# A fused decoder block in fp32: finer loads and stores, the weight loads on another queue, a new order, and bf16 products of constants that nobody reads

## The reference, cut to what matters

```
x = x + attention(layernorm(x))      # 16 query heads of 32, one shared key and value head, causal
x = x + xattn(layernorm(x), f, ctx)  # two int8-quantised products per batch element, silu between them
x = x + ffn(layernorm(x))            # 512 -> 1376 -> 512 gated, plus low-rank terms:
    gate = x@W_gate + lora(x) + sum_e w_e * (x@A_e)@B_e     # same for up and for down
    w    = top 2 of 8 experts by sigmoid(x@W_router) + bias, normalised
```

## Time and profile before

| | us |
|---|---|
| median of 3 runs | 1038.27 |
| lowest, highest | 1030.74, 1038.53 |
| the profiled execution, whole | 1036.64 |
| its span in the trace | 1034.7 |
| PE, PEld, DVE busy in the span | 931.2, 665.7, 618.7 |
| ACT, POOL busy in the span | 313.5, 248.5 |
| mean granted TensorE clock | 0.927 |

### The profile page before, as it was taken

How to read it: one execution, slowest core, us unless ns; L and a number is a source line. 1 busy time by engine, 2 the same in 40 slices (tenths; PEclk the granted TensorE clock), 3 DMA queues, 4 the chain that set the end, 5 groups by cost and what they waited for, 6 DMA issues and landing times.

```text
span 1034.7 us, 13134 instructions
## 1 busy us (share of the span) xinstructions
PE 931.2 (90%) x5214; PEld 665.7 (64%) x5214; DVE 618.7 (60%) x865; ACT 313.5 (30%) x496; POOL 248.5 (24%) x217
## 2 busy tenths in 40 slices
PE   1898898587998989999999899999979999779996
PEld 1665446454546767767677676766757787668884
DVE  2355667877568668676566686966467574532222
ACT  2423443254342313534314026343222422121110
POOL 3612331412524003123220040321303123001110
PEclk9957889697679999999999999999989999989999
DMA  7863682433645753356426733362354545445542
GB/s 262 284 209 106 241 275 74 117 113 109 235 156 215 208 178 120 123 201 241 173 72 186 208 115 129 124 236 98 127 191 153 190 163 202 153 150 199 178 163 87
DMA packets 42657, 174.98 MB, mean 169 GB/s; under 512 B 5148, under 2 KB 7964, under 8 KB 32612
## 3 DMA queue, kind: packets, MB, share of 16 engines
q1 hardware_dynamic: 42596, 174.14, 49.1%
HBM read 127.52 MB, written 33.75 MB: 156 GB/s over the span
## 4 chain that ended last, share of the span: by engine, by line
PE 72%; DVE 14%; issue 4%; SPq 4%; DMA 2%; ACT 2%; POOL 1%; POOLq 0%; DVEq 0%; ACTq 0%
PE ring L932 12%; PE ring L933 11%; PE ring L934 11%; PE av L1039 4%; PE slot L1025 4%; PE den L1039 3%; PE ring L1170 3%; PE slot L1005 3%; DVE negm L1288 3%; SPq L576 3%; PE slot L1108 2%; PE slot L932 2%; PE slot L934 2%; PE slot L1023 2%; PE slot L933 2%
## 5 line engine op out<-in xcount | busy, mean ns | idle before, releaser
L932 PE MATMUL ring<-xT_h,gu 128*128 128x512 f32 x352 | 144.7, 411 | 9.1 <-DMA gu<-gu_parts 8.5
L735 POOL TENSOR_TENSOR hd_l<-hd,hd_h 128x512 fp32r<-128x512 f32 x44 | 57.5, 1306 | 384.2 <-ACT hd_h L908 384.2
L1288 DVE TENSOR_REDUCE negm<-slot 128x4 f32<-128x512 f32 (+2 forms) x96 | 98.9, 1044 | 68.1 <-PE slot L1005 67.7
L933 PE MATMUL ring<-xT_l,gu 128*128 128x512 f32 x352 | 139.6, 397 | 0.0
L934 PE MATMUL ring<-xT_h,gu 128*128 128x512 f32 x352 | 139.5, 396 | 0.0
L810 ACT ACTIVATE probs<-slot 128x256 f32<-128x256 f32 (+3 forms) x128 | 85.6, 700 | 90.6 <-PE slot L1025 90.5
L932 PEld LDWEIGHTS ring<-xT_h,gu 128*128 128x128 f32 x352 | 67.6, 192 | 25.2 <-issue 10.9
L934 PEld LDWEIGHTS ring<-xT_h,gu 128*128 128x128 f32 x352 | 67.5, 192 | 15.1
L1025 PE MATMUL slot<-qst,kst 98*128 98x128 f32 (+3 forms) x256 | 77.1, 396 | 0.0
L933 PEld LDWEIGHTS ring<-xT_l,gu 128*128 128x128 f32 x352 | 67.8, 193 | 12.2
L1005 PE MATMUL slot<-kst,qst 96*128 96x128 f32 (+3 forms) x256 | 74.1, 401 | 0.0
(11 more groups left out here) (194 smaller groups left out, 1768.5 us busy)
## 6 DMA issues: line engine op xcount, KB each, us to landing
gu<-gu_parts SPq DMA_DIRECT2D x44, 1280.0 KB, 5.5
dn<-dn_parts SPq DMA_DIRECT2D x12, 1728.0 KB, 7.9
gu_parts<-gu SPq DMA_DIRECT2D x11, 1280.0 KB, 5.7
qst<-qT_h SPq DMA_DIRECT2D x64, 128.0 KB, 2.5
raw_gu<-gu SPq DMA_DIRECT2D x11, 640.0 KB, 7.4
dn_parts<-dn SPq DMA_DIRECT2D x11, 576.0 KB, 3.3
dn<-dn_parts SPq DMA_DIRECT2D x4, 1152.0 KB, 5.3
x_in<-x SPq DMA_DIRECT2D x4, 1024.0 KB, 6.3
```

Source lines behind the costliest of these rows:

```text
L735: pool.tensor_tensor(hd_l[:, i, :], hd[:, i, :], hd_h[:, i, :].bitcast(F32), ALU.subtract).then_inc(hd_lo.sem, 1)
L932: pe.matmul(out_, w_hi_, m_hi_, start=start, stop=False, skip_group_check=True)
L933: pe.matmul(out_, w_hi_, m_lo_, start=False, stop=False, skip_group_check=True)
L1288: dve.tensor_reduce(negm[:, h0:h0 + heads, qt].rearrange("p (a c) -> p a c", a=2), slots[SLOT["max", b, g, i]][:, :, 0:heads // 2 * n].rea ...
```

## The change

- **fill.** 94 new steps of PE alone issue 1 to 9 bf16 matmuls each of the identity with the 128x384 masks into the ring bank that comes next, 303 in all: 117 in 38 steps of FIRST, 136 in 37 of SECOND, none in STEADY, 50 in 19 of LAST. Nobody reads the result, as the next tenant of the bank starts its sum anew. A fill waits, as the next claim would, for the reader of that bank.
- **Loads.** The first load of x is two halves with a semaphore each, so are the later ones. c_loaded counts the constants and the masks alone; five small loads raise v_loaded, which is waited for where they are first used.
- **gu loads.** From tile 2 on they are issued by ACT, in step hid, behind its copy hd_h. Before, SP issued them.
- **Stores.** total is stored in four pieces of 256 KB, each when its rows are done.
- **Steps.** The low-rank products of gate and up are a step k = 4 of their own. w_turn and y stand behind the first four steps of gate of tile 0, not ahead of them, and w_turn takes a slot, not a ring bank.
- **Order.** The four strings are new.

```diff
@@ -78,6 +78,13 @@
         if place in self.left:
             eng.wait_ge(*self.left[place])
         self.left[place] = (signal.sem, value)
+        return self.places[place]
+
+    def upcoming(self, eng):
+
+        place = self.n % 2
+        if place in self.left:
+            eng.wait_ge(*self.left[place])
         return self.places[place]
 
 
@@ -207,16 +214,16 @@
     yield ("router", b)
     yield ("logits", b)
     yield ("route", b)
-    yield ("w_turn", b)
-    yield ("y", b)
     behind = []
     for f in range(FT):
         for name in ("gate", "up"):
-            for k in range(KT):
+            for k in range(KT + 1):
+                if f == 0 and name == "gate" and k == KT:
+                    yield ("w_turn", b)
+                    yield ("y", b)
                 yield (name, b, f, k)
                 if name == "up" and k == 1:
                     yield ("gated", b, f)
-        yield ("gu_load", FT * b + f + 2)
         yield ("hid", b, f)
         yield from behind
         behind = []
@@ -225,10 +232,11 @@
                 behind = [("ad", b, s)]
                 if s == len(SEGMENTS) - 1:
                     behind += [("yd", b)]
-                behind += [("down", b, s, tt, j) for tt in range(TT) for j in range(len(tiles))]
+                for tt in range(TT):
+                    behind += [("down", b, s, tt, j) for j in range(len(tiles))]
+                    behind += [("store", b, tt)] * (s == len(SEGMENTS) - 1)
                 behind += [("dn_load", len(SEGMENTS) * b + s + 1)]
     yield from behind
-    yield ("store", b)
 
 
 def preparation_steps():
@@ -240,36 +248,37 @@
         yield ("prep_gu", f)
         yield ("prep_dn", f)
         yield ("prep_out", f)
-    yield ("gu_load", 0)
-    yield ("gu_load", 1)
+    yield ("gu_first",)
     yield ("dn_load", 0)
 
 
 
 
 FIRST = (
-    "AAAAAAAAWWAAAAAAAAWAWAWAAAAAAAWWAAAAAAAAAAAAAAAAAAAAWAWAAAAWAAAAAAAAAAAAAWAAAAAAWWWAAAAAAAAAAAAAAAWAAAAAAAAWAA"
...
+    "41AAAA14AA1AAAAA19AAWAWAA1WAWA4AAA4AW1AA414A1AA1WWA1A4AAA4AAAAAAAAAAAA1AWA1AAAA9AWAWAAAAA94AAAAAAA1AWAWA4AAWAW"
...
 SECOND = (
-    "LAALLWLLALWAALLLAALLALWLAALLALLLLLLLALAALALLAAALLLAALLLWLWLLLWALLLLLLAAALAAALAAAAAALAAALLLAAAAAALAAALLALLLAALL"
...
+    "LLAAW4LLLAAWLLALAALLLWAL1AA41LALL9LLLLAAL99A9LALLA4LA9LA9LL4L1AALALLWLLL1LWWALL11L4LALLLAAALAA1AAAAALA11AALLAL"
...
 STEADY = (
-    "FFFFAFALFFLAFFAALAFFFFFAFLFFAAAFFAFALFFFFFAFAFFFFFFFLFFFLLFFFFFFFAFFALFAAFFFFAFFLLFLAFFFLFAFFFLALFFLFLFAFLLFFF"
...
+    "AFALFLFAFFFAFFAFAFFLAFLFFFALFFAAFAFFFAFFAFFFFLFFFFAFFLFFFFLFFAFFFFAFAFFLAFFFFALFLFFFFLFFALFAFFLALFLFALFFFLALLA"
...
 LAST = (
-    "FFFFFFLLLFFFFLLFFFFFFLLFFLFFFFLFFFFLFFLLFFFFFFLFFLFFFFLFLFLFFLFFFFLLFLLLFFFFFFFFLFFFFLLFLLFLFFFLFLFFFFLFFFLLFF"
...
+    "1FF1FLLFF1F414FFFF9LLFLFFLFFLFFFF1LFFFFFFFLFFFFLFFFFFLFFFLLFLLF1FFLFFLFFLFFFFLFLFLLFFFLFFLFFFLLLFFFLFFLLFFLFFF"
...
 
 
 def in_order():
     streams = {"A": [s for b in range(BATCH) for s in attention_steps(b)], "L": [s for b in range(BATCH) for s in layer_steps(b)],
                "F": [s for b in range(BATCH) for s in feed_forward_steps(b)], "W": list(preparation_steps())}
     left = {name: iter(steps) for name, steps in streams.items()}
-    order = [next(left[name]) for name in FIRST + SECOND + (BATCH - 2) * STEADY + LAST] + list(left["F"])
-    assert len(order) == sum(len(steps) for steps in streams.values())
+    order = [("fill", int(name)) if name.isdigit() else next(left[name])
+             for name in FIRST + SECOND + (BATCH - 2) * STEADY + LAST] + list(left["F"])
+    assert len([step for step in order if step[0] != "fill"]) == sum(len(steps) for steps in streams.values())
     return order
 
 
@@ -483,15 +492,16 @@
...
-            sp.dma_start(x_in[:, :, :], rows_of(x[0])).then_inc(x_loaded.sem, 16)
+            for h in range(2):
+                sp.dma_start(x_in[:, 2 * h:2 * h + 2, :], rows_of(x[0])[:, 2 * h:2 * h + 2, :]).then_inc(x_loaded[h].sem, 16)
             sp.dma_start(cst[:, :], ap["consts"][:, 0, :]).then_inc(c_loaded.sem, 16)
             sp.dma_start(masks[:, :, :], ap["consts"][:, 1:3, :]).then_inc(c_loaded.sem, 16)
...
-            sp.dma_start(bias_bc[:, :], ap["expert_bias"].partition_broadcast(P)).then_inc(c_loaded.sem, 16)
...
+            sp.dma_start(bias_bc[:, :], ap["expert_bias"].partition_broadcast(P)).then_inc(v_loaded.sem, 16)
...
@@ -515,16 +525,11 @@
                 if f + 2 < FT:
                     sp.dma_start(raw_dn[f % 2][:, :], ap["dn"][f + 2]).then_inc(raw_dn_loaded[f % 2].sem, 16)
 
-            def gu_load(n):
-                if n >= BATCH * FT:
-                    return
-                i, _, f = gu_tile(n)
-                if n < 2:
+            def gu_first():
+                for i in range(2):
                     for k in range(2):
                         sp.wait_ge(gu_stored[k].sem, 16 * raw_last[k])
-                else:
-                    sp.wait_ge(u_ps.sem, n - 1)
-                sp.dma_start(gu[i][:, :].bitcast(F32), gu_parts[f]).then_inc(gu_loaded[i].sem, 16)
+                    sp.dma_start(gu[i][:, :].bitcast(F32), gu_parts[i]).then_inc(gu_loaded[i].sem, 16)
 
             def dn_load(n):
                 if n >= BATCH * len(SEGMENTS):
@@ -624,21 +630,21 @@
...
-            def store(b):
-                sp.wait_ge(out_added.sem, out_added.at(b, TT * len(SEGMENTS)))
-                sp.dma_start(rows_of(out[b]), total[:, :, :]).then_inc(stored.sem, 16)
...
+            def store(b, tt):
+                sp.wait_ge(out_added.sem, out_added.at(b, TT * (len(SEGMENTS) - 1) + tt + 1))
+                sp.dma_start(rows_of(out[b])[:, tt, :], total[:, tt, :]).then_inc(stored.sem, 16)
...
@@ -743,7 +751,7 @@
...
-            act.wait_ge(c_loaded.sem, 16 * 7)
+            act.wait_ge(c_loaded.sem, 32)
...
@@ -886,7 +896,7 @@
...
             def w_turn(b):
...
-                act.activation(wxT[:, :], ring[RING["w_turn", b]][:, :], ACT.Copy).then_inc(wxT_ready.sem, 1)
+                act.activation(wxT[:, :], slots[SLOT["w_turn", b]][:, 0, :], ACT.Copy).then_inc(wxT_ready.sem, 1)
...
@@ -906,6 +916,10 @@
             def hid_(b, f):
                 act.wait_ge(hd_ready.sem, hd_ready.at(b, f + 1))
                 act.activation(hd_h[:, hid_slot(b, f), :], hd[:, hid_slot(b, f), :], ACT.Copy).then_inc(hd_hi.sem, 1)
+                n = FT * b + f + 2
+                if n < FT * BATCH:
+                    i, _, tile = gu_tile(n)
+                    act.dma_start(gu[i][:, :].bitcast(F32), gu_parts[tile]).then_inc(gu_loaded[i].sem, 16)
 
             def yd(b):
                 act.wait_ge(y_ready.sem, y_ready.at(b, 2))
@@ -924,9 +938,14 @@
         @block.tensor
         def _(pe):
             in_slots, in_ring = Tenants(slots, SLOT), Tenants(ring, RING)
-            pe.wait_ge(c_loaded.sem, 16 * 7)
+            pe.wait_ge(c_loaded.sem, 32)
             pe.wait_ge(masks_ready.sem, 2)
-            pe.wait_ge(consts_ready.sem, 5)
+
+            def fill(n):
+
+                ps = in_ring.upcoming(pe)
+                for _ in range(n):
+                    pe.matmul(ps[:, 0:3 * P], mask_bf[:, 0, :], mask_bf[:, :, :], start=True, stop=True, skip_group_check=True)
 
             def three(out_, w_hi_, w_lo_, m_hi_, m_lo_, start, stop):
                 pe.matmul(out_, w_hi_, m_hi_, start=start, stop=False, skip_group_check=True)
@@ -1148,10 +1169,10 @@
...
             def w_turn(b):
-                ps = in_ring.claim(pe, ("w_turn", b), wxT_ready, wxT_ready.at(b, 1))
+                ps = in_slots.claim(pe, ("w_turn", b), wxT_ready, wxT_ready.at(b, 1))
...
-                    mm = pe.transpose(ps[:, tt * P:(tt + 1) * P], wx[:, tt, :], ident)
+                    mm = pe.transpose(ps[:, 0, tt * P:(tt + 1) * P], wx[:, tt, :], ident)
...
@@ -1162,8 +1183,9 @@
                     held[name] = in_ring.claim(pe, (name, b, f), read, read.at(b, f + 1))
                     pe.wait_ge(gu_loaded[gu_tile(n)[0]].sem, 16 * gu_tile(n)[1])
                 ps = held[name]
-                three(ps[:, :], part[:, at:at + P], part[:, AT_LOW + at:AT_LOW + at + P], xT_h[:, k, :], xT_l[:, k, :], k == 0, False)
-                if k == KT - 1:
+                if k < KT:
+                    three(ps[:, :], part[:, at:at + P], part[:, AT_LOW + at:AT_LOW + at + P], xT_h[:, k, :], xT_l[:, k, :], k == 0, False)
+                else:
                     if f == 0:
                         pe.wait_ge(y_lo.sem, y_lo.at(b, y_n))
                     for low in range(2):
@@ -1253,7 +1273,7 @@
...
             def ln1_stats(b, h):
...
-                    dve.wait_ge(x_loaded.sem, x_loaded.at(b, 16))
+                    dve.wait_ge(x_loaded[h].sem, x_loaded[h].at(b, 16))
...
             def ln1_norm(b, h):
@@ -1496,7 +1518,7 @@
...
             def up(b, f, k):
-                if k < KT - 1:
+                if k < KT:
...
```

56 lines of the change are left out of this document (32 added, 24 removed).

## The result

The changed kernel takes **1023.12 us** (median of four runs, 1019.93 to 1026.54) against 1038.4 us (1030.74 to 1039.19) for the kernel before in the same session. The ratio is 0.987, with a 95% interval from 0.982 to 0.992. The prediction was 1014 us, with a range of 990 to 1032. The profiled execution took 1023.5 us against 1036.6, so 13.1 us are to be explained in the trace.

A forecast was written before the change was run, and what follows sets the result against it. PE bounds from 340 us on at full clock; before, some 94 us of its low clock are on the chain. 1036.6 -2.7 -21 +10 +1 -9 +3.2 -2 -1.8 = 1014.3, so 1014 us (990 to 1032).

The forecast's parts named there:

- Start, -2.7: At the kernel's start, attention weights can be copied earlier and POOL's subtractions move up, with all behind them: 2.7 us saved.
- Clock, -21: In the first stages, fills take away two thirds of the low-clock time, 31 us; 70% is kept: 21 us saved.
- fills on the path, +10: In FIRST and SECOND, a quarter of the fills' 41 us at full clock lies on PE's path: 10 us lost.
- my far end of -47: First stages: all 128 us go to the full clock, halving PE's 94 us on the chain: 47 us saved.
- Fills of LAST, +1: The 50 fills at waits of the routing and last down products take 8 us, 1 us of it on the path.
- Tile loads on ACT, -9: At two waits for tile 2's gu load, issue 2.3 us earlier and less low clock behind: 9 us saved.
- Tight loads in the last batch, +3.2: In batch 3, loads issued after ACT's copy make PE wait 0.8 us, four times: 3.2 us lost.
- Routing, -2: In batches 2 and 3, gate matmuls ahead of the turn shorten the routing step by 1 us each: 2 us saved.
- End, -1.8: After the last add, the last store is 256 KB instead of 1024 KB: 1.8 us saved.
- New order, 0: From 340 us on, the new order shifts no work between engines: zero, with 5 us either way.
- That the fills don't raise the clock: Rival for the first stages: clock stays low and fills cost little, 1028 us, or 1032 with less from gu loads; chance 0.2.
- That they cost more than they give: Rival: fills on PE's path at low clock in FIRST and SECOND make the kernel slower, 1066 us; chance 0.07.

The follow-up runs named there:

- the repeat: The changed kernel run once more, unedited: median 1022.79 us, ratio 0.990 to the kernel before.

## Why the prediction was right, point by point

**Start, -2.7: right for the place.** PE began 3.3 us earlier (that this reaches the end isn't shown: with the start's loads alone the ratio was 0.999, 0.995 to 1.002), and the parts of it are in the timeline as forecast (ACT's first copy of the attention weights at 9.74 us, POOL's subtractions at 10.57 for 13.78).

```profile
9.74 2.40 ACT L759 ACTIVATE wqkv_h<-wq_raw 128x576 fp32r<-128x576 f32 x4 [2.36 <-DMA wq_raw<-wqkv]
...
10.57 5.47 POOL L657 TENSOR_TENSOR wqkv_l<-wq_raw,wqkv_h 128x576 fp32r<-128x576 f32 x4 [8.66 <-ACT wqkv_h L759]
...
18.02 4.40 PE L977 MATMUL slot<-cst,x_in 128*128 128x128 f32 x16 [7.41 <-DVE x_in L1271]
```

**Clock, -21, and fills on the path, +10: the mechanism right, both sizes wrong.** I left a third of the low time and let DVE take back 30% of the gain. Against the same kernel without fills, 103.3 of 139.9 us went, three quarters, and PE's other work got 40 to 52 us shorter, about my far end of -47. DVE took nothing back that these rows show. On the other side I put a quarter of the fills' time, 10 us, on the path, where it was 19 to 32 us by the two counts above: they stand where the gap was to be, but they run for their full time once the gap is gone. The two misses offset each other: the net is -20.7 in that stretch, where I had -11. Against the kernel before, over the somewhat longer way to u0, it is -18.8.

By the rule of the Trainium skill that I weighed (TensorE: Matmul & The Clock Gate, section HAM oscillation), gaps bring the clock down and dense matmuls bring it back. Its -47 was nearer to what PE's other work gained than my -21; of the low time, three quarters went, nearer to my two thirds than to all. In the last batch the gap and the low clock behind it went together, as the rule has it. But 31 to 58 us of low clock stayed in the early stages of every kernel with 256 columns or more, and half as many fills again hardly moved them.

**Fills of LAST, +1: nothing.** From batch 2's router transposes to batch 3's, where these 50 run, it is 144.3 us in the kernel before, 144.3 in the changed one and 144.5 in the one without them.

**Tile loads on ACT, -9: wrong, the failed step of the sum.** "Which takes 4.6 of the 8.5 us of waits away" assumed that a transfer takes as long when it is issued earlier. The waits came to 5.12 + 3.75 = 8.87 us; none was saved. The issue was 3.6 us sooner than SP's, and the load beside w_raw took 12.29 us instead of 9.23. That w_raw has a large part in it was shown by moving it: 7.37 us. The section Key Constraints of the Trainium skill's page Trainium Kernel Development and Optimization, which says that all queues share 16 DMA engines and another queue saves only issue time, was right to doubt the gain, and even -5 was too much: in the kernel before, the load went out 9.7 us behind w_raw and took 8.53 us, here 5.2 us behind it, and shared the full engines for longer. PE's pace has a part, too. In the kernel without constant products, with the same queue, the two waits come to 5.08 us, 3.4 less than before. How much of that is the queue's stays open, since the kernel before with the start's loads alone, still on SP, has 6.40.

**Tight loads in the last batch, +3.2: less.** I had the issue 1.4 us behind the up half, after the copy hd_h. But both wait for DVE's hd alone:

```profile
909.20 0.69 DVE L1528 SCALAR_TENSOR_TENSOR hd<-gated,ring 128x512 f32<-128x512 f32 x1 [3.79 <-PE ring L1192]
909.92 0.63 ACT L918 ACTIVATE hd_h<-hd 128x512 fp32r<-128x512 f32 x1 [5.23 <-DVE hd L1528]
909.93 0.33 ACTq L922 DMA_DIRECT2D gu<-gu_parts  x1
...
951.29 0.47 PE L951 MATMUL ring<-xT_h,gu 128*128 128x512 f32 x1 [0.48 <-DMA gu<-gu_parts]
```

The DMA goes out 0.01 us behind the start of the copy that stands ahead of it in ACT's stream, 0.8 us behind the up half. The longest idle time of PE there is 0.48 us, and from the end of tile 0 to that of tile 10 it is 93.7 us against 92.1, 1.6 more in all.

**Routing, -2: none.** In batch 2 the wait shrank to 1.33 us, and from the router's transposes to u0 it is 22.9 us for 24.3. In batch 3, which has no fills, it was split as forecast, but the two parts are 1.71 and 2.79 us where the one wait was 4.65; the same way takes 25.1 us for 23.8. Both kernels have 6.8 us of low clock there, but PE is busy for 5.06 of them now and was for 3.04.

```profile
899.42 0.63 PE L1175 MATMUL slot<-cst,wx 128*128 128x128 f32 x4 [1.71 <-DVE wx L1500]
...
902.84 1.22 PE L1192 MATMUL ring<-y_g,gu 128*128 128x512 f32 x2 [2.79 <-DVE y_g L1511]
```

I had also placed LAST's fills "at waits of the routing and the last down products"; they end before the last batch.

**End, -1.8: right, but not what the stretch gave.** The last add ends at 1019.24, 2.5 us ahead of the end, and there were 4.8. But 6.8 us of low clock now lie at 1006.9 behind a wait of 2.38 us, where the kernel before had the same wait and no low clock. The timeline, and then the table by stretch:

```profile
1005.62 0.50 PE L1209 MATMUL ring<-hd_h,dn 128*128 128x512 f32 x1 [2.38 <-POOL hd_l L743]
...
1018.55 0.69 DVE L1556 TENSOR_TENSOR total<-ring,total 128x512 f32<-128x512 f32 x1 [1.35 <-PE ring L953]
```

```profile
1006.90:1013.70 6.80, 5.92 (x15) 4.14 (x14) 2.26 (x4) 0.63 (x1) 0.00 (x0) 0.50 0.10 39
```

**New order, 0: 4 us worse, within the 5 allowed.** From u0 to the end the kernel without any fills needs 680.7 us against 676.3, and the changed kernel 685.4 (682.1 in the repeat). So some 4 us belong to the order, the tile loads or both. The changed kernel with its loads on SP needs 685.7 us, the same as with ACT, which speaks for the order; the old order was not run with the new loads, so it isn't shown.

**The rivals.** That the fills don't raise the clock fell. That they cost more than they give turned out to be a matter of amount: half as many again cost about what they give. The sum of that rival has a slip: the other terms (2.7 + 9 + 2 + 1.8 - 3.2) give 12.3 us, not 15, so its time would have been 1068 and not 1066.

## What to carry to other kernels

Matmuls that nobody reads can pay where the clock falls behind short gaps, but they are bought with path time. Size them by the idle time that is there, compare against the same kernel with none, and expect a flat best (256 and 384 columns the same here) with a loss right behind it.

Before a load is moved to a freer queue, look at the DMA share in the stretch where it will run. If it is near 1, an earlier issue may bring little (0.4 us at the place here). Splitting the buffer, so that a part can be loaded earlier, brought more (some 5 us by the two places), and still took its time from the moves that share the engines.

A wait that was harmless in one execution (2.38 us at the end of the kernel before) can have 6.8 us of low clock behind it in the next. In the few idle places of the PE-bound tail the constant products cost less than they gave in the profiles: 133.1 us for the last batch against 137.7 and 135.0.

## What the runs showed that I had not expected

The split into low and high clock varies between executions of one kernel, and the time with it: 1019.7 to 1031.2 us in twelve runs of the changed kernel, at mean clocks of 0.977 to 0.960. A DMA issue in ACT's stream did not wait for the activation ahead of it to end: in 40 of the 42 tile loads it stands 0.01 us behind its start, the copy being 0.63 us long. Two loads that overlap do not each keep their time: 1280 KB took 5.5 us as a median, 7.37 beside the moves of heads, and 12.29 beside these and 1 MB more (10.2 to 12.3 in seven kernels where the 1 MB goes out 5.1 to 5.3 us ahead).
